# Softmax sums in an attention stage: the last tile's add moves from TensorE's sum to VectorE, and attention's steps are due one step earlier in the planned order

## What is computed

```python
x = x * s1[:, None, :]
x = (x - mu) * rsqrt(var + EPS_IN)
q = heads(einsum('bsh,oh->bso', x, q_weight) * q_dc[:, None, :])     # k alike
v_flat = einsum('bsh,oh->bso', x, v_weight) * v_dc[:, None, :] * s2[:, None, :]
attn = softmax(einsum('bhqd,bhkd->bhqk', q, k) * scale)
out = einsum('bhqk,bhkd->bhqd', attn, v) -> (B, S, H)
out = einsum('bsh,oh->bso', out, w_weight) * w_dc[:, None, :]
skip = einsum('bsh,oh->bso', v_flat, u_weight) * u_dc[:, None, :]
return out + skip
```

## Time and profile before

| | |
|---|---|
| Time, median of 3 runs | 6457.05 us (6448.9 to 6458.57) |
| The profiled execution: its own time | 6452.4 us |
| its span, first to last instruction | 6450.6 us |
| mean granted TensorE clock | 0.962 |
| attention's last multiply (line 1083) starts | 3341.7 us |
| busy: TensorE / VectorE / ScalarE / GpSimd | 6002.0 / 4564.4 / 2348.0 / 3206.0 us |

### The profile page before, as it was taken

The page is one execution under the profiler, slowest core; times in us unless marked ns, Lnnn a source line. Parts: engine busy times, 40 slices in busy tenths (PEclk is TensorE's granted clock), DMA queues, the critical chain, the costliest instruction groups (busy, mean ns, idle before and its releaser), DMA issues. The chain is left out here.

```text
span 6450.6 us, 73170 instructions
## 1 busy us (share of the span) xinstructions
PE 6002.0 (93%) x24000; PEld 2740.8 (42%) x24000; DVE 4564.4 (71%) x5830; ACT 2348.0 (36%) x4460; POOL 3206.0 (50%) x2625
## 2 busy tenths in 40 slices
PE   7999999999999999999986869999999999999998
PEld 4444444444444444444434324444444444444343
DVE  4655656555565655555535999998999999998984
ACT  2444444444444444443444323333232323233111
POOL 1776666766657666676655232424334342424313
PEclk7999999999999999999987989999999999999999
DMA  2332313323233231332214234444444344444433
GB/s 87 82 86 74 97 52 96 89 74 94 53 99 89 74 92 45 105 85 64 84 54 132 62 98 107 128 108 113 121 119 126 99 135 99 129 105 114 124 92 113
DMA packets 411564, 613.29 MB, mean 95 GB/s; under 512 B 58768, under 2 KB 189968, under 8 KB 410672
## 3 DMA queue, kind: packets, MB, share of 16 engines
q1 hardware_dynamic: 374320, 558.24, 31.3%
q10 hardware_dynamic: 36864, 50.38, 3.0%
HBM read 305.31 MB, written 201.38 MB: 79 GB/s over the span
## 5 line engine op out<-in xcount | busy, mean ns | idle before, releaser
L1125 POOL TENSOR_TENSOR acc<-acc,prob 128x512 f32<-128x512 f32 x1536 | 1906.6, 1275 | 960.6 <-PE bank L815 728.0
L1055 DVE TENSOR_REDUCE mx<-bank 128x1 f32<-128x512 f32 x2048 | 1314.7, 684 | 588.4 <-PE bank L785 583.7
L2064 DVE SCALAR_TENSOR_TENSOR g<-xps,bd,g 128x1024 f32<-128x1024 f32 x1024 | 1312.7, 1282 | 156.9 <-PE xps L1794 83.8
L948 ACT ACTIVATE prob<-misc 128x512 f32<-128x512 f32 x1496 | 842.7, 597 | 852.4 <-PE misc L802 690.0
L1794 PE MATMUL xps<-sx,spread 128*128 128x512 f32 x2048 | 886.8, 519 | 181.1 <-DVE g L2064 164.4
L785 PE MATMUL bank<-khat,qhat 96*128 96x512 f32 x2048 | 989.7, 534 | 40.0 <-DVE mx L1055 20.5
L2070 DVE TENSOR_SCALAR g<-g,lim 128x1024 f32<-128x1024 f32 x1024 | 881.0, 860 | 32.3
L802 PE MATMUL misc<-qhat,khat 98*128 98x512 f32 x1679 | 724.1, 461 | 58.7 <-ACT prob L948 42.1
L1794 PEld LDWEIGHTS xps<-sx,spread 128*128 128x128 f32 x2048 | 357.0, 195 | 707.5 <-DVE g L2064 387.7
L1808 PE MATMUL yps<-g,cexp 128*32 128x512 f32 x4096 | 603.5, 641 | 0.1
L785 PEld LDWEIGHTS bank<-khat,qhat 96*128 96x128 f32 x2048 | 390.7, 196 | 433.7 <-issue 298.8
(11 more groups left out here) (220 smaller groups left out, 6781.2 us busy)
## 6 DMA issues: line engine op xcount, KB each, us to landing
sx<-scratch_xhl SPq DMA_DIRECT2D x512, 128.0 KB, 4.9
scratch_dx<-dx SPq DMA_DIRECT2D x64, 512.0 KB, 2.7
scratch_xhl<-xhi SPq DMA_DIRECT2D x64, 512.0 KB, 4.2
scratch_xhl<-xn SPq DMA_DIRECT2D x64, 512.0 KB, 4.6
scratch_y<-ysb SPq DMA_DIRECT2D x512, 64.0 KB
dx_t<-scratch_dx SPq DMA_DIRECT2D x59, 512.0 KB, 6.2
y_t<-scratch_y SPq DMA_DIRECT2D x59, 512.0 KB, 3.9
xt_n<-in_x SPq DMA_DIRECT2D x112, 256.0 KB, 3.0
```

Source lines behind the costliest of these rows:

```text
L948: act.activation(to, bank[m][:, 0:QC], ACT.Exp, scale=SCALE).then_inc(sem[f"act_m{m}"], 1)
L1055: dve.tensor_reduce(self.mx2[:, h * TT + qt, c:c + 1], bank[m][:, 0:QC], AX.X, ALU.max).then_inc(sem[f"dve_m{m}"], 1)
L1125: pool.tensor_tensor(self.acc[:, a, h, :], self.acc[:, a, h, :], self.prob[:, (n % 2) * GH + h, :], ALU.add).then_inc(sem["pool_acc"], 1)
L2064: dve.scalar_tensor_tensor(self.g[:, t % 4, :], self.xps[t % 2][:, :], self.bd[:, i % 2, tl:tl + 1], self.g[:, (t - 1) % 4, :], ALU.mult, ...
```

## The change

Four edits, all in the attention stage.

1. `N` loses its first loop: it is four matmuls (eight instructions) on `acc` alone, and its cost in the plan falls from 1.95 to 1.1. It waits for `A` of the last tile.
2. A piece `A` exists for `kt` = 7 as well, on VectorE, with a cost of 0.7 in the plan and the semaphore `dve_norm`. It waits for `E` of its head and step and for GpSimd's `A` of the same head for `kt` = 6, and adds `prob` to `acc`. Its due is t = n - 0.5 like the other `A`.
3. `E` that reuses the last tile's slot waits for that `A` instead of `N`. `R`, which waited for every `dve_norm` ahead of it, now waits for the `D` of the chunk before by name, since `dve_norm` now counts the adds too.
4. Every piece of `attend` is due one step earlier than before: `u * n_steps + t - 1.0`.

```diff
         def put(t, *a, **k):
             put_(*a, **k)
-            out[-1]["due"] = u * n_steps + t
+            out[-1]["due"] = u * n_steps + t - 1.0
...
-                if 0 < kt < TT - 1:
+                if kt:
+
+                    add = ("POOL", 1.28) if kt < TT - 1 else ("DVE", 0.7)
                     for h in range(GH):
-                        put(n - 0.5, "POOL", 1.28, ("A", u, k, h), (("E", u, k, h),) + (
-                            (("C", u, k - 1),) if kt == 1 else (("A", u, k - 1, h),)), [("pool_acc", 1)])
+                        put(n - 0.5, *add, ("A", u, k, h), (("E", u, k, h),) + (
+                            (("C", u, k - 1),) if kt == 1 else (("A", u, k - 1, h),)),
+                            [("pool_acc" if kt < TT - 1 else "dve_norm", 1)])
...
-                put(n, "PE", 1.95, g, tuple(("A", u, c * TT + TT - 2, h) for h in range(GH)), [("pe_m{m}", 1)], take=SIDE, group=g)
+                put(n, "PE", 1.1, g, tuple(("A", u, c * TT + TT - 1, h) for h in range(GH)), [("pe_m{m}", 1)], take=SIDE, group=g)
...
-                n = c * TT + TT - 1
                 for h in range(GH):
-                    self.of_bank(w, "act", ("S", u, n, h), ("E", u, n, h))
-                    pe.matmul(bank[m][h * DH:(h + 1) * DH, 0:QC], self.ones32[:, :], self.prob[:, (n % 2) * GH + h, :],
-                              start=True, stop=False)
-                for h in range(GH):
-                    w.wait_ge(sem["pool_acc"], plan.after("pool_acc", ("A", u, n - 1, h)))
+                    w.wait_ge(sem["dve_norm"], plan.after("dve_norm", ("A", u, c * TT + TT - 1, h)))
                     mm = pe.matmul(bank[m][h * DH:(h + 1) * DH, 0:QC], self.ones32[:, :], self.acc[:, a, h, :],
-                                   start=False, stop=True)
+                                   start=True, stop=True)
...
-                        if v % TT == TT - 1:
-                            sums = ("N", old[0], old[1] // TT)
-                            self.of_bank(w, "pe", sums, sums)
-                        else:
-                            w.wait_ge(sem["pool_acc"], plan.after("pool_acc", ("A", *old, h)))
+                        added = "dve_norm" if v % TT == TT - 1 else "pool_acc"
+                        w.wait_ge(sem[added], plan.after(added, ("A", *old, h)))
...
-                w.wait_ge(sem.get("dve_norm"), plan.before("dve_norm", p))
+                if u or c:
+                    old = (u, c - 1) if c else (u - 1, self.NQ - 1)
+                    w.wait_ge(sem["dve_norm"], plan.after("dve_norm", ("D", *old)))
...
+            elif kind == "A" and at[1] % TT == TT - 1:
+                u, n, h = at
+                c, kt, a = self.step(u, n)
+                self.of_bank(w, "act", ("S", u, n, h), ("E", u, n, h))
+                w.wait_ge(sem["pool_acc"], plan.after("pool_acc", ("A", u, n - 1, h)))
+                dve.tensor_tensor(self.acc[:, a, h, :], self.acc[:, a, h, :], self.prob[:, (n % 2) * GH + h, :],
+                                  ALU.add).then_inc(sem["dve_norm"], 1)
```

More of the change, by code:

```diff
@@ L381, in attend @@
                     v -= 2 if v % TT == 0 else 0
-                    last = ("N", v // n_steps, v % n_steps // TT) if v % TT == TT - 1 else None
-                    old = lambda h: (("C", v // n_steps, v % n_steps), last or ("A", v // n_steps, v % n_steps, h)) if v >= 0 else ()
+                    old = lambda h: (("C", v // n_steps, v % n_steps), ("A", v // n_steps, v % n_steps, h)) if v >= 0 else ()
                 for h in range(GH):
@@ L1115, in gpsimd @@
                                    ALU.mult).then_inc(sem["pool_w"], 1)
-            elif kind == "A":
+            elif kind == "A" and at[1] % TT < TT - 1:
                 u, n, h = at
```

## The result

The changed kernel took 6488.92 us in the median of 4 runs (6486.29 to 6496.45), the kernel before 6457.64 us beside it; the ratio is 1.0055, 95% interval 1.0042 to 1.0067. The forecast was 6410 us, range 6360 to 6475. The first rival, VectorE's queue holding TensorE up, had given 6482 us at 16 holds.

A forecast was written before the change was run, and what follows sets the result against it. TensorE was taken to bound attention, busy 479 of 500 us in its middle. The terms -55.0 - 10 + 17 + 0 + 0.7 = -47.3 us gave 6405.1, plus 4.65 to the median: 6410 us, range 6360 to 6475.

The forecast's parts named there:

- The first rival: Attention: VectorE's new adds wait for GpSimd and hold up TensorE, 5.6 us a hold, 6482 us at 16 holds; chance 0.16.
- Part 3: 256 new adds on VectorE: their work hidden beside TensorE's, three holds of its queue at about 5.6 us each, +17 us.
- Part 1: The sum on TensorE: eight instructions fewer a chunk, 0.86 us in each of 64 chunks, counted in full, -55.0 us.
- Part 2: TensorE's wait at the sum for GpSimd's last adds, 31.2 us over 64 chunks: a third of the upper gain, -10 us.
- The sign that I had named: Profile after, VectorE's new adds: a mean over 1.1 us would be the exclusion with GpSimd at work in most adds.
- Part 4: Attention's pieces due one step earlier: all work remains, taken as 0 us, bounds -46 and +62.
- The end of attention: Last chunk: an add of 0.7 us comes between GpSimd's last add and the final sum, +0.7 us once.
- The second: Rival, no change: side work slips behind attention and the next unit waits, or saved time becomes waiting; 6454 us, chance 0.12.
- The third, more than the sum: Rival in attention: all 31 us of waiting goes, no holds, earlier dues win 46 us; 6325 us, chance 0.09 below 6370.

The follow-up runs named there:

- e6: The changed kernel with waits both ways, in the plan too, so VectorE's adds and GpSimd's work never overlap: 6444.0 us.
- e9: As e6, but VectorE's adds wait only for GpSimd's adds ahead of them, not for its scaling and multiplies: 6404.5 us.
- e3: The changed kernel with VectorE's new piece a maximum over prob alone (one SBUF input, one column out), last tile left out of the denominator: 6367.6 us.
- e5: The changed kernel without VectorE's new piece, the sum waiting for GpSimd's add of the tile before, last tile left out of the denominator: 6354.9 us.
- e2: The kernel before with only attention's dues one step earlier: 6393.1 us.
- e8: The kernel before with dues one step earlier for attention's pieces on TensorE only: 6405.7 us.
- e12: The kernel before with only attention's dues three steps earlier: 6502.8 us.
- m1: Separate kernel computing nothing of the reference: GpSimd runs of eight instructions, mostly with one VectorE operation ready behind the second; two-SBUF-input add beside GpSimd's adds 1.43 us.

## Why the prediction was wrong

**The step that failed is Part 3, the 256 adds on VectorE**, "I take three holds, +17". It was the right mechanism with a price for a hold (5.6 us) that the runs bear out (121 us over 24 long adds are 5.0 each), and a count that was far off: 24 adds take over 2.6 us, and the second input costs 121 us. The count failed for two reasons. I took line 2077's longest case (1849 ns) as the bound of one add, 1.1 us; the longest was 7.8 us above the undisturbed 0.68. And I argued that maxima aren't pressing when the last tile comes. At a unit's end, where 17 of the 24 are, the sum itself is next on TensorE and waits for the adds.

Two things in the kernel before spoke against that bound. The first is in its code. The scan's plan marks line 2077's pieces and GpSimd's with `port=True`, and `Order.run` starts a piece so marked no earlier than the end of the last marked piece of the other engine. So only 46 of the 384 operations of line 2077 overlap a GpSimd instruction, 28 of them with a length over 0.9 us. Attention's pieces carry no such mark, and the change gave its new add none; e6 and e9 do. The second is in the earlier trace rows. Line 1005 took 3.41 us for 0.16 us of work because GpSimd held it, over two further adds:

```profile
1498.94 8.69 POOL L1125 TENSOR_TENSOR acc<-acc,prob 128x512 f32<-128x512 f32 x7
```

GpSimd's run ends at 1507.63, the operation at 1507.65. The place from which I took the price of a hold was a hold by GpSimd in attention itself, longer than one instruction, and I didn't ask what had made it long. Line 2077's longest case isn't quite the rest of one GpSimd add either, as I had read it:

```profile
3432.28 1.85 DVE L2077 SCALAR_TENSOR_TENSOR cv<-xr,wconv,cv 128x512 f32<-128x512 f32 x1 [2.29 <-ACT cv L1908]
3432.31 2.95 POOL L2193 TENSOR_TENSOR xn<-xn,affine 128x512 f32<-128x512 f32 x2
```

It started 0.07 us before the end of one GpSimd instruction and ended 0.55 us behind the whole of the next, which had started after it.

The SBUF page of the Trainium skill (SBUF — State Buffer, Who interferes with whom) says that whichever comes first has the pair of ports for its whole instruction and the other blocks, that copies on VectorE can take part and reductions never do. The kernels by themselves agree (1.43 to 1.77 us, 0.69 with a PSUM input, 1.25 for the copy), and so does e3 (687 ns at most). Attention goes beyond it, with up to 8.51 us over seven GpSimd instructions, and there the measurement decides.

Point by point:

- **Part 1**, -55.0 for eight instructions a chunk: right in sign, too large; 38 us measured (e5 against e2, which also drops the waits for the last tile). TensorE was busy for 96% of the stretch by the modelled spans, but 17 of the 55 us don't appear in the time; which wait took them wasn't looked for.
- **Part 2**, -10 for the wait at the sum: not borne out. In the changed kernel TensorE's matmuls wait 48.3 us for VectorE's adds at the sum over all chunks and the weight loads 62.4. The 31.2 us before are both together, 3.7 us of them before matmuls and 27.5 before weight loads, so there was less to win than I had read. The expected saving can't be told apart from Part 1 in e5, which keeps GpSimd's wait.
- **Part 3**, +17: +13 for the work itself (costed at nothing, hidden) and +121 for the second SBUF input. The sign that I had named, a mean of over 1.1 us "in most adds", misled: the mean was 1.21 us, from 44 of 256 adds.
- **Part 4**, 0 for the dues: -62. The lower bound was -46 and fell short. The sum had no term for an order that keeps ScalarE and GpSimd fed, nor for holds that the order makes or takes away; e8 puts 49 us of it on TensorE's ties.
- **The end of attention**, +0.7: in the last chunk VectorE's add of head 0 takes 4.1 us, and its last add ends at 3372.43, 2.4 us behind GpSimd's last (3370.07), so the price was some 1.7 us more than I had put down.

The experiments form a chain from the kernel before over e2, e5 and e3 to the change: -62 - 38 + 13 + 121 = +34, against 6488.9 - 6457.6 = +31 measured. Such a chain closes whatever its steps are, so this doesn't confirm them; the 3 us between are the kernel before from batch to batch. Taken in another order the steps have other sizes: the moved add cost 116 us with the old dues and 96 with the new.

Of the rivals the first is what happened, in place and mechanism, at a chance of 0.16 that was too low. That its 6482 us at 16 holds lies so near the 6488.9 measured is luck: by its own working 24 holds give 134 - 65 = +69, 6526 us, and the 62 us that the dues gave, which it didn't have, brought the time down again. The second didn't happen at one step (e2) and shows in part at three (e12). The third, more than the sum, was right that the dues win something, 46 us in it and 62 measured, and wrong that nobody holds VectorE.

## What to carry to other kernels

Before an elementwise operation with two SBUF inputs goes to VectorE, look at what GpSimd does at that moment, not at how idle VectorE is on the mean: an engine that was 42% free lost more here than the move could win. Where the two must meet, give VectorE's operation an input in PSUM or order the two by a semaphore (here that won 84 us back, but not a gain over leaving the add where it was), and bound its length by GpSimd's longest run without a gap, not by one instruction. When an operation on a few columns takes microseconds, ask which engine held it before its length is used as a price. And take a change of priorities in a list schedule as an edit of its own: here it was worth more than the work that was removed, and it was the only part worth keeping.

## What the runs showed of the hardware

- VectorE's add with two SBUF inputs (0.68 us undisturbed) lasted up to 8.51 us in attention. All 44 that began beside GpSimd ended some 0.55 us after the end of a GpSimd instruction, and outside the two chunks with turns that was the last of a run without a gap; GpSimd's adds kept their length meanwhile (1.344 us at most). Reductions with one SBUF input (662 to 687 ns) and the add with one in PSUM (677 to 692 ns) were never held; a copy was (1.25 us in m1, one case).
- Operations of 128x8 were held as well: one with one SBUF input (`TENSOR_SCALAR`, 0.16 us) for 3.4 us seven times of seven in the kernel before, one with two (0.17 us) for up to 7.48 us in the changed one. They ended 0.02 to 0.03 us after a GpSimd add.
- By themselves the two engines took turns, 72 times out of 72: 1.66 to 1.77 us for VectorE, up to 1.72 us for GpSimd. Three kernels didn't find what makes the difference.
- A GpSimd add of a tensor to itself takes 1.04 us, of two tensors 1.26 us, 128x512 float32 each.
